# One kernel of differential attention and a ternary feed-forward layer: the projections run in the score products' row halves, the row sums move into the product banks

## The reference

```python
# attention, on y = layernorm(x)
qkv = y @ w_qkv; q, k, v -> 16 heads of 32; q1, q2 and k1, k2 are the halves of 16
a1 = softmax(q1 @ k1.T / sqrt(32)); a2 = softmax(q2 @ k2.T / sqrt(32))
lam = exp(lq1 . lk1) - exp(lq2 . lk2) + 0.8
o = (a1 - lam * a2) @ v
o = o / rms(o) * norm_w * 0.2
x = x + (heads and rows of o transposed together) @ wo
# feed-forward, on y = layernorm(x): ternary weights with a scale per row
h = bitlinear(y, w_fc) + gate * (y @ v.T @ fast_b.T @ u.T)
x = x + bitlinear(relu(h) ** 2, w_proj)
```

## Time and profile before

| | |
|---|---|
| median of three runs | 3755.79 us |
| profiled execution | 3755.76 us, its span 3754.0 us |
| mean granted TensorE clock | 0.996 |
| PE / weight loads / DVE / ACT / POOL busy | 99% / 55% / 84% / 74% / 16% |
| attention pairs 0 to 63 (first to last score) | 101.3 to 2751.3 us |

### The profile page before, as it was taken

One profiled execution on the slowest core, in us unless ns is written; L12 is line 12 of the kernel. 1 busy time (PEld: TensorE's weight loads), 2 busy tenths in 40 slices (PEclk: granted clock), 3 DMA queues, 4 the chain that ended last, 5 costly groups with the idle time before them and its releaser, 6 DMA issues.

```text
span 3754.0 us, 57605 instructions
## 1 busy us (share of the span) xinstructions
PE 3705.5 (99%) x21704; PEld 2053.0 (55%) x21704; DVE 3152.0 (84%) x2927; ACT 2796.3 (74%) x3629; POOL 584.1 (16%) x269
## 2 busy tenths in 40 slices
PE   7999999999999999999999999999999999999999
PEld 6444444444444444444444444444468888888887
DVE  6899999999999999999999999988865555555554
ACT  4798888888888888888888989888863333333333
POOL 0101101023434343223223201210010000000000
PEclk9999999999999999999999999999999999999999
DMA  7544444445444444554554444534340101010010
GB/s 239 134 102 105 103 105 105 102 100 111 102 99 104 107 106 99 112 115 102 110 114 112 100 100 103 133 82 114 77 152 23 45 23 46 23 46 23 29 40 23
DMA packets 255350, 344.56 MB, mean 92 GB/s; under 512 B 118000, under 2 KB 142576, under 8 KB 254000
## 3 DMA queue, kind: packets, MB, share of 16 engines
q1 hardware_dynamic: 251504, 324.43, 36.6%
q0 software_dynamic: 3392, 15.73, 1.3%
q10 hardware_dynamic: 128, 0.03, 0.0%
HBM read 198.55 MB, written 131.07 MB: 88 GB/s over the span
## 4 chain that ended last, share of the span: by engine, by line
PE 88%; DVE 7%; issue 3%; DMA 1%; ACT 1%; SPq 0%; ACTq 0%; DVEq 0%
PE ps L875 22%; PE ps L850 16%; PE ps L940 13%; PE ps L995 12%; PE ps L786 9%; DVE acc L1632 5%; PE ps L926 4%; PE ps L789 4%; PE ps L896 3%; PE ps L945 2%; PE ps L758 1%; PE ps L1031 1%; PE ps L909 1%; PE ps L1016 1%; ACT pr L1261 0%
## 5 line engine op out<-in xcount | busy, mean ns | idle before, releaser
L1261 ACT ACTIVATE pr<-ps 128x1024 f32<-128x1024 f32 x2048 | 1989.8, 1029 | 257.0 <-PE ps L850 249.5
L1632 DVE TENSOR_TENSOR acc<-acc,pr 128x2048 f32<-128x2048 f32 x768 | 1780.9, 2319 | 40.3 <-ACT pr L1261 10.5
L875 PE MATMUL ps<-pr,vst 128*32 128x512 f32 x8192 | 1010.5, 599 | 0.3 <-DMA vst<-v_scratch 0.3
L850 PE MATMUL ps<-qst,kst 50*128 50x512 f32 x4096 | 781.9, 457 | 9.3 <-ACT pr L1261 6.9
L850 PEld LDWEIGHTS ps<-qst,kst 50*128 50x128 f32 x4096 | 337.1, 184 | 655.1 <-ACT pr L1261 460.1
L875 PEld LDWEIGHTS ps<-pr,vst 128*32 128x32 f32 x8192 | 213.4, 109 | 447.0 <-issue 436.6
L1430 ACT ACTIVATE rb<-ps,scf 128x512 f32<-128x512 f32 x228 | 157.0, 689 | 352.9 <-PE ps L945 352.9
L995 PE MATMUL ps<-tP,hh_ 128*128 128x512 f32 x1024 | 400.3, 391 | 0.6 <-DVE hl_ L1836 0.6
L995 PE MATMUL ps<-tP,hl_ 128*128 128x512 f32 x1024 | 399.5, 390 | 0.0
L786 PE MATMUL ps<-xt,wqh 128*128 128x512 f32 x1024 | 376.8, 419 | 3.0 <-DVE xt L1521 3.0
L940 PE MATMUL ps<-yh,tT 128*128 128x512 f32 x896 | 351.2, 392 | 0.0
(11 more groups left out here) (177 smaller groups left out, 3790.0 us busy)
## 6 DMA issues: line engine op xcount, KB each, us to landing
qst<-q_scratch SPq DMA_DIRECT2D x128, 256.0 KB, 4.6
kst<-k_scratch SPq DMA_DIRECT2D x128, 256.0 KB, 7.0
q_scratch<-stg SPq DMA_DIRECT2D x112, 256.0 KB
k_scratch<-stg SPq DMA_DIRECT2D x112, 256.0 KB
qst<-q_scratch SPq DMA_DIRECT2D x128, 128.0 KB, 4.9
kst<-k_scratch SPq DMA_DIRECT2D x128, 128.0 KB, 7.7
vst<-v_scratch SPq DMA_DIRECT2D x128, 128.0 KB, 4.6
xr<-in_L_attn_x_dram SPq DMA_DIRECT2D x64, 256.0 KB
```

The costliest lines, as they stand in the source:

```text
L850: ins = e.matmul(ps[:, 2 * c + hh, :], kst[rows, r, j, t * 128:(t + 1) * 128], qst[rows, r, j, c * 512:(c + 1) * 512], start=True, stop=True)
L875: ins = e.matmul(ps[32 * c4:32 * c4 + 32, 4 + j, :], vst[:, r, t, 32 * hh:32 * hh + 32], pr[:, sl, c, hh, :], start=(t == 0), stop=(t == 7 ...
L1261: e.activation(pr[:, sl, c, :, :], ps[:, 2 * c:2 * c + 2, :], ACT.Exp, scale=SCALE).then_inc(s_exp, 1)
L1632: e.tensor_tensor(acc[:, j, :], old, new, ALU.add).then_inc(s_add, 1)
```

## The change

It rearranges what fills the steps of the pairs with projections, and moves parts of the output's chain.

- `pe_couple`: for P < 56, the first two tiles of a pair are made together in steps 0, 1 and 2, and from pair 2 on the third tile together with the output product of pair P - 2 in steps 4, 5 and 6. Every product of 128 rows becomes two of 64 rows. A couple is one half of the one tile beside the other half of the other tile, in the two row halves, into banks 6 and 7; there are 24 couples, 8 a step. After twelve, the halves are exchanged, and PE waits until the twelfth couple has been written (`s_half`). In pairs 0 and 1 the third tile runs as before, 4 products a step. Steps 3 and 7 have no projection.
- The row sums go into the product banks 4 and 5 themselves (`4 + j`), one step later (d = 6, and d = 2 of the next pair). For that ACT first copies the raw product out (`act_raw`, into `sq` or, times minus lambda, into `ot`).
- `first_half`, `join_halves` (two operations), `scale_heads`, `output_high` and `output_low` run on POOL, in this order within an iteration: layernorm, `scale_heads(P - 2)`, `output_high(P - 2)`, `join_halves(P - 1)`, `output_low(P - 2)`, magnitudes or ternary weights, `first_half(P)`, magnitudes. Before, the high part was ACT's and the others DVE's.
- The output's transposes go to step 7 (bank 4), those of the layernormed rows to step 3 (bank 5). DVE keeps the sum of squares, the last add and the tiles' low parts and bounds, at other places; SP's stores and loads follow.
- In pair 56 the low-rank products start one step earlier and alternate between banks 7 and 6. From pair 56 on, the output product runs in full height in steps 6 and 7.
- The flag (a rare case of large scores) takes one group of matmuls instead of two. `pe_down(0, 0)` stands before the last sum, and its inputs are prepared in pair 63.

The core of the diff:

```diff
-PIECES = {0: (0, 0, 6), 1: (0, 6, 12), 2: (1, 0, 8), 3: (1, 8, 12), 4: (2, 0, 6), 5: (2, 6, 12)}
+WAVES = (0, 8, 16, 24)
...
+        def tile_half(e, T, bk, u, h, first, last):
+
+            C, i = kind_of(T)
+            k, part = divmod(u, 3)
+            rows = slice(64 * h, 64 * h + 64)
+            w = (wqh, wql, wqh)[part]
+            xx = (xhi(C), xhi(C), xlo(C))[part]
+            if i < 8:
+                m0 = TILES[i] * 128
+                return e.matmul(ps[:, bk, :], w[rows, k, m0:m0 + 128], xx[rows, k, :], start=first, stop=last)
...
+        def pe_couple(e, P, c, n0, n1):
+
+            T = 24 + 3 * P + 2 * c
+            C, i = kind_of(T)
+            if n0 == 0 and c == 0:
+                if P:
+                    tile_read(e, T - 1)
+                    if P < 3:
+                        tile_read(e, T - 2)
+                    else:
+                        e.wait_ge(s_x2v, P - 2)
...
+            elif n0 == 0:
+                tile_read(e, T - 2)
+                tile_read(e, T - 1)
+                e.wait_ge(s_oth, P - 1)
...
+            for n in range(n0, n1):
+                h, u = divmod(n, 12)
+                if n == 12 and n0 < 12:
+                    e.wait_ge(s_half, 2 * P - 1 + c if P >= 2 else P + 1)
+                if c and n == 8:
+                    e.wait_ge(s_otl, P - 1)
+                a = tile_half(e, T, 6, u, h, n == 0, n == 23)
+                if c:
+                    b = out_half(e, u, 1 - h, n == 0, n == 23)
+                else:
+                    b = tile_half(e, T + 1, 7, u, 1 - h, n == 0, n == 23)
+                if n == 11:
+                    b.then_inc(s_half, 1)
...
         def pe_sum(e, X, j):
             e.wait_ge(s_add, n_add(X, j, 7))
...
+            e.wait_ge(s_rw, 2 * X + j + 1)
             for hh in range(2):
                 for c in range(2):
                     c4 = 2 * hh + c
-                    t = e.matmul(ps[32 * c4:32 * c4 + 32, sum_bank(X, j), :], ones[:],
+                    t = e.matmul(ps[32 * c4:32 * c4 + 32, 4 + j, :], ones[:],
...
-                    if d == 1 and P:
+                    if d == 2 and P:
                         pe_sum(e, P - 1, 1)
-                    if d == 5:
+                    if d == 6:
                         pe_sum(e, P, 0)
...
+                    if P < LOWP and d % 4 < 3:
+                        if d < 4:
+                            pe_couple(e, P, 0, WAVES[d], WAVES[d + 1])
+                        elif P >= 2:
+                            pe_couple(e, P, 1, WAVES[d - 4], WAVES[d - 3])
...
+        def act_raw(e, X, j):
+            e.wait_ge(s_pv, 16 * X + 8 * j + 8)
...
+                e.activation(sq[:], ps[:, 4, :], ACT.Copy).then_inc(s_rw, 1)
...
+                e.activation(ot[:], ps[:, 5, :], ACT.Identity, scale=neglam).then_inc(s_rw, 1)
...
+        def first_half(e, X):
             e.wait_ge(s_rex, 2 * X + 1)
...
+            e.wait_ge(s_rw, 2 * X + 1)
+            e.tensor_tensor(rl[:, 0, :], sq[:], rl[:, 0, :], ALU.mult).then_inc(s_pt, 1)
+
+        def join_halves(e, X):
+            e.wait_ge(s_rex, 2 * X + 2)
+            e.wait_ge(s_rw, 2 * X + 2)
+            e.tensor_tensor(ot[:], ot[:], rl[:, 1, :], ALU.mult).then_inc(s_pt, 1)
+            e.wait_ge(s_pt, 2 * X + 2)
+            e.tensor_tensor(ot[:], ot[:], rl[:, 0, :], ALU.add).then_inc(s_ot, 1)
+
+        def scale_heads(e, X):
...
+            e.tensor_tensor(heads, heads, ms[:, 2, :].unsqueeze(2).broadcast_to([128, 16, HD]), ALU.mult).then_inc(s_on, 1)
+
+        def output_high(e, X):
...
+            e.tensor_scalar(oth[:], on[:].rearrange("p (k n) -> p k n", k=4), 1.0, None, ALU.mult).then_inc(s_oth, 1)
+
+        def output_low(e, X):
+            e.wait_ge(s_oth, X + 1)
+            e.tensor_tensor(otl[:], on[:].rearrange("p (k n) -> p k n", k=4), oth[:], ALU.subtract).then_inc(s_otl, 1)
...
             pe_pv(e, NSLOT - 1)
+            pe_down(e, 0, 0)
             pe_sum(e, NPAIR - 1, 1)
```

More of the change, by code:

```diff
@@ L808, in load_flag, with pe_flag @@
+        def pe_flag(e, b):
+            bk = 6 if b else 5
+            e.wait_ge(s_flv, 6 * b + 2)
+            if b:
+                tile_read(e, 24 + 3 * (b * NP - 1))
+            else:
+                e.wait_ge(s_xtl, 10)
+            for m in range(4):
+                t = e.matmul(ps[0:1, bk, 8 * m:8 * m + 8], nmx[:, 24 + m:25 + m], ind[:], start=True, stop=True)
+            t.then_inc(s_flp, 1)
         def load_flag(e, b):
@@ L1308, in act_posts, with act_out, act_out_square @@
-        def act_posts(e, P, d, half):
-            for a in range(3, 0, -1):
-                act_post(e, P - a, 8 * (a - 1) + d, half)
+        def act_out(e, X, bk):
+            e.wait_ge(s_tr, X + 1)
+            if X:
+                e.wait_ge(s_otl, X)
+            else:
+                e.wait_ge(s_lamv, 7)
+            e.activation(on[:], ps[:, bk, :], ACT.Copy).then_inc(s_raw, 1)
+        def act_out_square(e, X, bk):
+            if X:
+                e.wait_ge(s_ssq, X)
+            e.wait_ge(s_pt, 2 * X + 3 if X < NPAIR - 1 else 2 * NPAIR)
+            e.activation(sq[:], ps[:, bk, :], ACT.Square).then_inc(s_osq, 1)
@@ L1675, in dve_posts, with dve_out_sum @@
[L1675 to L1682 removed]
+        def dve_out_sum(e, X):
+            e.wait_ge(s_osq, X + 1)
+            if X:
+                e.wait_ge(s_rmln, X)
+            e.tensor_reduce(ms[:, 0, :], sq[:].rearrange("p (g d) -> p g d", d=HD), AX.X, ALU.add).then_inc(s_ssq, 1)
@@ new lines, in vector_program @@
+                        if d == 4 and more:
+                            dve_bound(e, 24 + 3 * P + half)
+                        if (d, half) == (7, 0) and more:
+                            dve_low(e, 26 + 3 * P, 6)
+                            if P >= 2:
+                                dve_out(e, P - 2)
+                        if (P, d, half) == (0, 1, 1):
+                            dve_part_stats(e, -1)
+                        if (P, d, half) == (1, 1, 0):
+                            dve_part_stats(e, 0)
```

625 lines of the change are left out of this document (319 added, 306 removed).

## The result

The changed kernel takes 3853.32 us (median of 4 runs, 3849.46 to 3855.5) against 3755.59 in the same session (4 runs): a ratio of 1.0258 with a 95% interval of 1.024 to 1.0276. It is slower by 98 us. The prediction was 3778, with a range of 3695 to 3845; the measured time lies above it. The profiled execution has a span of 3853.7.

A forecast was written before the change was run, and what follows sets the result against it. It took PE (99% busy, steps no shorter than about 4.82 us) as the bound, DVE close second. Span 3754.0 + 29 for pairs - 7 for single places = 3776, plus 1.8 around it: 3778 us, range 3695 to 3845.

The forecast's parts named there:

- (a): Couples, eight a step in six steps: each at 0.23 us, so such a step takes 4.82, 4.83 with roundings.
- (b): Steps 3 and 7 lose their products but stand on the floor: 4.82 and 4.91 us, whatever transposes they hold.
- E: Rival on steps 3 and 7: content counts, no floor, 3.8 us there and 38.97 a pair, total 3624; chance 0.05.
- (c): Half exchange in steps 1 and 5: PE waits for its own twelfth couple, 0.32 us, twice a pair.
- (d): Row sums, now in steps 2 and 6: still 2 x 0.86 us a pair, without waits for the last add.
- (f): DVE loses five short operations, together 2.8 us a pair, leaving DVE 37.3 without them.
- (g): POOL's new operations delay DVE's adds beside them: DVE pays 3.8 us, 41.1 in a plain pair; no stall.
- (h): Pair times from DVE at 41.1 beside PE at 41.07: 41.4 plain, 42.4 in pairs 17 to 32, 41.8 after; +29 us.
- (i): Single places: pair 56 -4 us, end of attention -2, the flag's second matmul -1, other pairs and the rest 0.
- B: Rival: PE decides, POOL's delays fall into DVE's idle time, every pair 41.07 us, total 3738; chance 0.22.
- D: Rival: POOL's delays all uncovered, DVE at 42.0, 43.3 and 42.7 us a pair, total 3820; chance 0.11.
- D2: Rival: POOL locks DVE out for its whole operation, DVE pays 6.2 us a pair, total 3908; chance 0.05.

The follow-up runs named there:

- e9_noswap: e7_fixed with the couples kept in the same row halves for all 24 units (no swap) and the flag's limit at 1e30: 3797.12 us, ratio 1.0111.
- e2_short: The changed kernel with POOL's six operations on 64 of 512 columns from pair 2 to 61, output incomplete: 3772.14 us, ratio 1.0035.
- e6_both: The changed kernel with DVE's subtracts of the second tile and of the transposed part each one add earlier: 3828.91 us, ratio 1.0192.
- e10_gather: e7_fixed, but every fourth part's statistics three adds earlier and their short ACT and DVE operations in the pair before: 3764.67 us, ratio 1.0024.
- e14_back: e10_gather with five of the output chain's six operations back on DVE, the first half ahead of add 14: 3759.22 us, ratio 1.0008.
- e4_places: The changed kernel with ACT's variance operations behind step 0's third exp and step 4 waiting only for DVE's first flag read: 3824.7 us, ratio 1.0177.
- e7_fixed: e6_both and e4_places together, plus the flag's evaluation one add earlier and an output sum moved to the end of pair 56: 3802.09 us, ratio 1.0121.
- e13_short: e11_split with POOL's six operations on 64 of 512 columns from pair 2 to 61: 3739.24 us, ratio 0.9951.
- e11_split: e10_gather with the second score group of steps 1 and 5 between the twelfth and thirteenth couple: 3760.61 us, ratio 1.0011.

## Why the prediction was wrong

(a) Couples: right. The timeline of PE in step 1 of pair 51; a couple is two matmuls, so x4 are two couples and x2 is one:

```profile
2298.30 0.63 PE L838 MATMUL ps<-xt,wqh 64*128 64x512 f32 x4
2298.77 0.39 PE L838 MATMUL ps<-xt,wql 64*128 64x512 f32 x2
2299.00 0.95 PE L838 MATMUL ps<-xt,wqh 64*128 64x512 f32 x4
2299.79 0.39 PE L838 MATMUL ps<-xt,wql 64*128 64x512 f32 x2
```

2298.77 to 2299.00 is the interval of 0.23; a step with eight takes 4.82 to 4.84 (4.83 was said). Rival F is out.

(b) Right: steps 3 and 7 are 4.86 and 4.91. Content does not count, E is out. The rule of the Trainium skill, page "TensorEngine Tiling (Array Packing)", section "Key Properties", was cited for E: a change of tiling mode drains TensorE. A change costs what the earlier trace rows show, but steps 3 and 7, with fewer of them, got no shorter than the 4.82 and 4.91 of before.

(c) Right: the row that holds the swap takes 0.95 instead of 0.63, 0.32 more, and e9_noswap gives 0.34. C is out by this wait.

(d) Right: 6.02 = 4.83 + 0.86 + 0.33, and no sum waits for an add in attention. **PE's own sum of 41.07 stands**: e2_short has plain pairs of 41.1, e6_both too.

(e) ACT: right for its load (74% both times), wrong for one place: its operation on the variance, moved to the head of step 0, waits for DVE.

(f) Right, as far as the runs show: with an eighth of the chain left on POOL DVE has 37.2 (37.3 was said without any).

(g) Right in kind, too large in size: DVE's 40.2 less (f)'s 37.3 is 2.9, and e2_short gives 3.0 for seven eighths, instead of 3.8. The longest add takes 3.20, the 0.9 more of the estimate; the two of 6.07 together have 1.4 more, the first of the rows above (2.70) 0.4, and the one at 2305.36 nothing. No run shows by itself the 0.4 that a short operation was said to cover. The Trainium skill, page "SBUF — State Buffer", section "SBUF: two separate sides", would have it at 6.2 by the prediction's estimate, had POOL held every add for its whole length: the runs show half of that. The Trainium skill, page "Perfetto Trace Analysis", section "Optimizing Scalar/DVE Operations", warns that moving work between DVE and GpSimd might not help; e10_gather against e14_back bears it out, 5 us. "No stall" of POOL's low part was right for the changed kernel.

(h) **This is the step that failed.** The time of a pair was taken as a bound of totals, and the wait of PE for DVE's subtracts was put at nothing. It took a pair as the larger of two sums, 41.07 for PE and 41.1 for DVE, and added 0.3 for unevenness: 29 us over pairs 2 to 55. They lost 89.3, with DVE at 40.2. What decides is not DVE's total but where it stands when PE needs a bank. In pair 51 it came to L1673 at 2314.16; five of POOL's six operations run one behind the other from 2300.74 to 2315.37, just ahead of and beside the two subtracts that free banks 7 and 5. Of the 1.4 us of delay in that stretch PE sees 1.0, and the idle time that DVE has elsewhere doesn't give it back: there it waits for ACT's exps, which wait for PE. The text had the fact (banks free "only about 1 us ahead of need") under what would make it wrong, and gave it neither a price nor a chance. Worked out afterwards in its own terms, 2 x 0.88 for two adds beside POOL less 1 us of cover is 0.8 a pair; measured is 1.0. On 41.07 that is 54 x 41.87 - 2229 = +32, about the +29 that (h) gave by totals: so even the right road with these sizes would have fallen short. The rest, 89.3 - 54 = 35 us, is the same lateness at DVE's other results that somebody waits for, which (h) held at nothing: the gather in every fourth pair (17 of it, e4_places) and the flag (most of what is left). The stages went wrong with it: pairs 17 to 32 are no longer than the others.

(i) Pair 56 gained 1.3, not 4. End of attention: the last sum no longer waits, but the down products wait 4.2 us for their DVE input instead (2.3 + 0.6 before): +1.8, not -2. The last pairs of the batches lose 20.7, some 7 of it by step 4 as everywhere, so the flag costs about 13 instead of saving 1: a wait of PE on a result of DVE was put right behind the stretched adds. Pair 57: 4.1 instead of 0; its first up product (L1022) waits 2.1 us for an output sum of DVE (L1751), and with that sum moved in e7_fixed the pair is at -0.2.

The rivals: B's condition, POOL's delays in idle time, did not hold. e13_short comes out at B's price, 3738, with the chain cut short, but by luck in part: it also has the split score groups, which take up to 11 us from PE's own sum. D and D2 lie on either side of the result, but by a total of DVE that was not there (40.2 a pair, not 42 and more).

The loss, shown part by part: step 4 of the plain pairs 35 us (e6_both), every fourth pair 31 (e10_gather), flag pairs 18 (e7_fixed), pair 57 4 (e7_fixed). With these orders mended the change is worth about nothing: 1.0024 (1.0014 to 1.0034) with POOL's chain, 1.0008 with DVE's. PE's own sum of 41.07 a pair, 11 us less than before over pairs 2 to 55, is reached by neither: they take 7 and 4 us more than before there.

Open: why e13_short's 21 us of contention fall on pairs 21 to 38 above all wasn't followed up (in pairs 17 to 32, where the magnitudes run, DVE is busy 98.1% in e11_split and 90.5% in e13_short, so a full DVE is likely but not shown step by step), nor was the start, where the first scores come 1 to 6 us later from run to run.

## What to carry to other kernels

When work is handed to another engine, add up not only both engines' totals but, for each result that a third engine waits for, the time from its input to its due time with all that now stands ahead of it; here a short operation one place too late in a queue cost about 1 us in nearly every one of 54 pairs, three times over (the subtracts L1673 and L1665, the first half). An engine that is 94% busy can be the cause of a wait, and after each mended order the next due operation has to be looked at. A wait that is moved (to free one queue) makes somebody else's first operation later: follow it to the last queue, DMA issues included.

## What the runs showed of the hardware

- DVE's add of 2048 columns takes 2.28 us alone, and mostly 2.7 to 3.2 beside POOL's operations of 128x512 (2.70 for one and 6.07 for two in pair 51; 3.20 at most). POOL's two-input ones take 1.5 to 3.3 in that pair, where L1900 takes 1.27 alone. The exchange is about even: 3.0 us a pair on DVE in contention for seven eighths of six operations, 2.8 (the prediction's reading) for five as its own work, and 5 us between e10_gather and e14_back.
- Row-half couples run at 0.23 us each, like one full product; a matmul that has to wait for PE's own previous result in the same bank costs 0.32 to 0.34.
- A stand of PE of 4.8 us came with a granted clock of 0.68 over the 10.7 us around it; the step before and the one behind it had 1.00.
